# Attention tower on one core: every product on 64 rows by 32 columns of TensorE, and a step of an attend and of a piece beside each pair of scores

## What is computed

```python
h = gelu(layernorm(x.reshape(8, 1500, 80) @ W.T + b) * gamma + beta)      # 256 features
z = layernorm(h)
Q, K, V = (z @ W.T + b for each of q, k, v), split into 16 heads of 16 features
attn = softmax(Q @ K.T / 4)                                               # 1500 x 1500 for each head
h = h + (attn @ V) @ Wo.T + bo
out = h + layernorm(layernorm(h)) * ln_g + ln_b                           # the expert layer: 8 // 16 = 0 tokens a head
```

## Time and profile before

| | us |
|---|---|
| median of 3 runs | 2458.41 |
| the profiled execution's own time | 2458.36 |
| its span | 2456.6 |
| TensorE busy | 2237.6 |
| ScalarE busy | 2155.3 |
| VectorE busy | 920.3 |
| GpSimd busy | 371.5 |

### The profile page before, as it was taken

The page is one execution under the profiler, slowest core; times in us unless marked ns, Lnnn a source line. Parts: engine busy times, 40 slices in busy tenths (PEclk is TensorE's granted clock), DMA queues, the critical chain, the costliest instruction groups (busy, mean ns, idle before and its releaser), DMA issues.

```text
span 2456.6 us, 47924 instructions
## 1 busy us (share of the span) xinstructions
PE 2237.6 (91%) x19500; PEld 669.8 (27%) x19500; DVE 920.3 (37%) x2075; ACT 2155.3 (88%) x2332; POOL 371.5 (15%) x495
## 2 busy tenths in 40 slices
PE   4589999999999999999999999999999999998892
PEld 1222223222232223222232222322222222222221
DVE  7442235432354334532345233542335332330114
ACT  0098999989999899998999899998999989999991
POOL 2211102211021111210112110211112110110002
PEclk7799999999999999999999999999999999999996
DMA  2311221222112222212212221222222122111101
GB/s 71 107 37 40 66 67 41 57 66 65 50 40 66 64 66 49 57 48 58 74 40 52 70 66 40 50 62 60 69 54 50 41 65 67 47 44 39 33 6 32
DMA packets 109922, 133.62 MB, mean 54 GB/s; under 512 B 32263, under 2 KB 89670, under 8 KB 109694
## 3 DMA queue, kind: packets, MB, share of 16 engines
q1 hardware_dynamic: 107158, 128.64, 20.8%
q10 hardware_dynamic: 2536, 1.83, 0.3%
HBM read 55.16 MB, written 61.44 MB: 47 GB/s over the span
## 4 chain that ended last, share of the span: by engine, by line
issue 47%; PE 27%; ACT 10%; POOL 8%; DVE 3%; POOLq 1%; DMA 1%; SPq 1%; DVEq 0%; ACTq 0%
PE PS L853 12%; PE PS L829 8%; PE PS L790 5%; ACT prob L489 4%; ACT prob L486 4%; POOL sq L380 2%; POOL Y L388 2%; ACT prob L494 2%; POOL rs L390 2%; POOLq L389 1%; PE PS L799 1%; PE PS L774 1%; DVE z L550 1%; DVE HL L568 1%; POOL rs L367 1%
## 5 line engine op out<-in xcount | busy, mean ns | idle before, releaser
L853 PE MATMUL PS<-prob,Vst 125*32 125x500 f32 x9216 | 1131.4, 593 | 0.2 <-ACT prob L489 0.2
L494 ACT ACTIVATE prob<-PS 125x1000 f32<-125x1000 f32 x768 | 776.4, 1011 | 135.9 <-PE PS L829 134.6
L829 PE MATMUL PS<-QA,KA 64*125 64x500 f16 x4608 | 769.0, 406 | 84.5 <-ACT prob L489 45.7
L486 ACT ACTIVATE prob<-PS 125x1000 f32<-125x1000 f32 x768 | 775.3, 1010 | 80.4 <-PE PS L829 80.3
L489 ACT ACTIVATE prob<-PS 125x1000 f32<-125x1000 f32 x768 | 784.4, 1021 | 0.0
L829 PEld LDWEIGHTS PS<-QA,KA 64*125 64x125 f16 x4608 | 255.9, 131 | 861.6 <-ACT prob L486 413.6
L853 PEld LDWEIGHTS PS<-prob,Vst 125*32 125x32 f32 x9216 | 219.6, 108 | 424.6 <-issue 242.5
L566 DVE TENSOR_SCALAR HL<-PS,b_qk 128x500 f16<-128x500 f32 x96 | 70.9, 739 | 504.1 <-PE PS L790 427.7
L790 PE MATMUL PS<-zT,w_qk 128*32 128x500 f32 x1536 | 197.4, 596 | 8.9 <-DVE Osb L611 7.6
L380 POOL TENSOR_TENSOR sq<-HL 128x2000 bf16<-128x2000 f16 x24 | 84.5, 3522 | 752.4 <-DVE HL L568 752.4
L611 DVE COPY Osb<-PS 128x500 f32<-128x500 f32 x96 | 65.0, 677 | 257.5 <-PE PS L853 257.5
(11 more groups left out here) (79 smaller groups left out, 955.0 us busy)
## 6 DMA issues: line engine op xcount, KB each, us to landing
qk_halves_scratch<-HL SPq DMA_DIRECT2D x384, 125.0 KB
QA<-qk_halves_scratch SPq DMA_DIRECT2D x64, 375.0 KB, 5.0
KA<-qk_halves_scratch SPq DMA_DIRECT2D x64, 375.0 KB, 7.2
oT<-On SPq DMA_DIRECT2D x384, 31.2 KB, 2.0
out<-Y SPq DMA_DIRECT2D x24, 500.0 KB
X<-in_x SPq DMA_DIRECT2D x8, 468.8 KB, 7.9
thin<-Osb SPq DMA_DIRECT2D x96, 7.8 KB
Den<-thin SPq DMA_DIRECT2D x96, 7.8 KB
```

What stands on the lines that cost most here:

```text
L486: act.activation(prob[0:T, 6 * p:6 * p + 2, :], PS[0:T, 0:2, 0:QC], ACT.Exp, scale=scl)\
L494: act.activation(prob[0:T, 6 * p + 4:6 * p + 6, :], PS[0:T, 4:6, 0:QC], ACT.Exp, scale=scl)\
L829: last = pe.matmul(PS[0:T, bank, 0:QC], KA[rows, G % 2, h // 2, t * T:(t + 1) * T], QA[rows, G % 2, h // 2, c * QC:(c + 1) * QC], start=Tr ...
L853: last = pe.matmul(PS[lo:lo + 2 * HD, 6 + n % 2, 0:QC], Vst[:, b % 2, t, g * HG + j, :], prob[0:T, (HG * t + j) % 12, :], start=(t == 0), ...
```

## The change

All products except the transpositions and the norm sums now use 64 rows by 32 columns of the array, so eight run at once. An attend becomes two **steps** of eight matmuls with 250 queries: in step 0 the upper 64 rows work on one half of the queries and the lower 61 on the other, each into its own bank, and in step 1 they change places. A projection becomes four steps (two input halves, two places), the values, the output and the token embedding two. Each of these results now lies in two banks, one half of its columns in each. The table counts **windows** of one pair of scores (24 in a unit) instead of rounds of three, and gives each step a window of its own. Scores use banks 0 to 3, two pairs; attends and pieces use 4 and 5 or 6 and 7 in turn. Two new semaphores, `s_ph` and `s_stp`, make the second step of an attend or piece wait for the first, which wrote the bank that it adds to.

TensorE:

```diff
-            def attend(n, t):
-                for j in range(HG):
-                    last = pe.matmul(PS[lo:lo + 2 * HD, 6 + n % 2, 0:QC], Vst[:, b % 2, t, g * HG + j, :],
-                                     prob[0:T, (HG * t + j) % 12, :], start=(t == 0), stop=(t == NT - 1))
-                last.then_inc(s_pv, 1)
+            def attend(n, t, step):
...
+                if step:
+                    pe.wait_ge(s_ph, at(s_ph, NT * n + t + 1))
+                elif NT * n + t > 0:
+                    pe.wait_ge(s_pv, at(s_pv, NT * n + t))
+                for lower in range(2):
+                    a = (step + lower) % 2
+                    rows = slice(64, T) if lower else slice(0, 64)
+                    for j in range(HG):
+                        lo = 2 * HD * j
+                        last = pe.matmul(PS[lo:lo + 2 * HD, bank + a, 0:QC // 2], Vst[rows, b % 2, t, g * HG + j, :],
+                                         prob[rows, (HG * t + j) % 12, a * QC // 2:(a + 1) * QC // 2],
+                                         start=(t == 0 and step == 0), stop=(t == NT - 1 and step == 1))
+                last.then_inc(s_pv if step else s_ph, 1)
...
-                    last = pe.matmul(PS[0:T, bank, 0:QC], KA[rows, G % 2, h // 2, t * T:(t + 1) * T],
-                                     QA[rows, G % 2, h // 2, c * QC:(c + 1) * QC], start=True, stop=not exact_max)
+                        last = pe.matmul(PS[lo:hi, bank, 0:QC], KA[rows, G % 2, h // 2, t * T + lo:t * T + hi],
+                                         QA[rows, G % 2, h // 2, c * QC:(c + 1) * QC], start=True, stop=not exact_max)
...
-                for r in range(PER):
-                    R = R0 + r
-                    if R > 0:
-                        pe.wait_ge(s_ex, at(s_ex, 3 * R))
-                    scores(n, 6 * r + 4, 2, exact_max)
-                    pe.wait_ge(s_ex, at(s_ex, 3 * R + 1))
...
+                for k in range(WIN):
+                    w = WIN * n + k
+                    if w > 0:
+                        pe.wait_ge(s_ex, at(s_ex, w))
+                    if k < WIN - 1:
+                        scores(w + 1, exact_max)
...
+                    if k >= 2:
+                        attend(n, (k - 2) // 2, k % 2)
+                    elif n > 0:
+                        attend(n - 1, NT - 1, k)
+                    beside(b, u, k)
```

The table (two of its lines), and VectorE's finish, which now comes three windows after the take:

```diff
+    OFFSETS = {"tok": (0, 1), "turn": (0,), "qk": (0, 1, 3, 4), "val": (0, 1), "norm": (0,), "flag": (0,), "out": (0, 1)}
+    place(6, "qk", (4, 5), (11, 6), (18, 7))
+    place(7, "val", (4, 4), (7, 5), (10, 6), (13, 7))
...
+                            take_out(pb, i)
+                            finish.append((k + 3, pb, i))
```

The start and the end of the program. Before the first unit only four pairs of banks rotate, and the sums over the weights wait until the tokens are out of PSUM; after the last unit VectorE finishes one tile behind the take:

```diff
+                    pe.wait_ge(s_free, at(s_free, NT // 2))
...
-                for e in range(4, 8):
-                    take_out(B - 1, e, USE["out", B - 1, e] % 6)
-                    finish_out(B - 1, e)
-                invert(B * NU - 1)
-                normalise(B * NU - 1)
-                for e in range(8, NT):
-                    take_out(B - 1, e, USE["out", B - 1, e] % 6)
-                    finish_out(B - 1, e)
+                for e in range(CT, NT):
+                    take_out(B - 1, e)
+                    if e > CT:
+                        finish_out(B - 1, e - 1)
+                    if e == CT + 1:
+                        invert(B * NU - 1)
+                    if e == CT + 2:
+                        normalise(B * NU - 1)
+                finish_out(B - 1, NT - 1)
```

More of the change, by code:

```diff
@@ L11, in audio_tower @@
     RF, D = tok_wT.shape
+    RH = RF // 2
     NT, T = x.shape[2], x.shape[3]
@@ L27, in audio_tower @@
     BOUND = 60.0
[L28 to L89, removed]
+    WIN = NT * HG // 2
+    assert NU == NT and WIN == 24 and KR == 64
+    OFFSETS = {"tok": (0, 1), "turn": (0,), "qk": (0, 1, 3, 4), "val": (0, 1), "norm": (0,), "flag": (0,), "out": (0, 1)}
+    PLAN = {(u, k): [] for u in range(NU) for k in range(WIN)}
+    def place(u, what, *at):
+        for k, i in at:
+            for step, off in enumerate(OFFSETS[what]):
+                PLAN[u, k + off].append((what, i, step, step + 1 == len(OFFSETS[what])))
@@ new lines, in audio_tower @@
+    place(0, "out", (4, 4), (9, 5), (19, 6))
+    place(0, "tok", (14, 2))
+    place(1, "out", (4, 7), (14, 8))
+    place(1, "tok", (9, 3), (19, 4))
+    place(2, "out", (4, 9), (14, 10), (19, 11))
+    place(2, "tok", (9, 5))
+    place(3, "turn", (4, 0), (6, 1))
+    place(3, "qk", (9, 0), (16, 1))
+    place(4, "qk", (4, 2), (14, 3))
+    place(4, "val", (11, 0), (21, 1))
+    place(5, "val", (4, 2), (7, 3))
+    place(5, "turn", (10, 2), (12, 3))
+    place(5, "norm", (14, 0))
+    place(5, "qk", (16, 4))
@@ new lines, in audio_tower @@
+    place(6, "qk", (4, 5), (11, 6), (18, 7))
+    place(7, "val", (4, 4), (7, 5), (10, 6), (13, 7))
+    place(7, "turn", (16, 4), (18, 5))
+    place(7, "norm", (20, 1))
+    place(8, "qk", (4, 8), (11, 9), (18, 10))
+    place(9, "qk", (4, 11))
+    place(9, "val", (11, 8), (14, 9), (17, 10), (20, 11))
+    place(10, "norm", (4, 2))
+    place(10, "flag", (8, 0))
+    place(10, "tok", (12, 0), (18, 1))
+    place(11, "out", (4, 0), (9, 1), (14, 2), (19, 3))
+    assert all(len(steps) < 2 for steps in PLAN.values())
@@ new lines, in values @@
+            def values(b, i, step, swap):
+                bank, t = pair(USE["val", b, i]), (i % CT) * T
+                begin("val", b, i, step)
+                for c in range(KC):
+                    for lower in range(2):
+                        j = (swap + lower) % 2
+                        rows = slice(64 * lower, 64 * lower + 64)
+                        for lo, hi in blocks(T):
+                            last = pe.matmul(PS[lo:hi, bank + j, 0:D // 2], zT[rows, c, t + lo:t + hi],
+                                             w_v[rows, c, j * D // 2:(j + 1) * D // 2], start=(step == 0 and c == 0),
+                                             stop=(step == 1 and c == KC - 1))
+                end("val", b, i, step, last)
@@ new lines, in output @@
+            def output(b, e, step, swap):
+                bank = pair(USE["out", b, e])
+                if step == 0:
+                    pe.wait_ge(s_os, at(s_os, 64 * (b * NU + (NG - 1) * NC + e // CT + 1)))
+                begin("out", b, e, step)
+                for c in range(KC):
+                    for lower in range(2):
+                        j = (swap + lower) % 2
+                        rows = slice(64 * lower, 64 * lower + 64)
+                        for lo, hi in blocks(T):
+                            last = pe.matmul(PS[lo:hi, bank + j, 0:D // 2], oT[rows, c, e * T + lo:e * T + hi],
+                                             w_o[rows, c, j * D // 2:(j + 1) * D // 2], start=(step == 0 and c == 0),
+                                             stop=(step == 1 and c == KC - 1))
+                end("out", b, e, step, last)
```

479 lines of the change are left out of this document (256 added, 223 removed).

## The result

The changed kernel takes **2652.66 us** (median of 4 runs, 2637.40 to 2657.69), where the kernel before takes 2457.94 (4 runs): ratio 1.078, 95% interval 1.076 to 1.080. It is slower by 195 us where I forecast faster by 173. The profiled execution has a span of 2654.8.

What follows compares the result with a forecast made beforehand. TensorE and ScalarE equally loaded, TensorE's late scores costing 210 us. Start 120, gelus and table loads 35, exponentials 2041, lateness 50 and end 37 made a 2283 span, plus 1.8 outside: 2285 us, range 2245 to 2410.

Steps and rivals of the forecast that it cites:

- More instructions: TensorE's 1568 rows a unit, at 6 ns a row as in a burst, hide behind the array; cost set at nothing.
- Rows cost more than they fill: Rival: TensorE's sequencer can't keep up, deciding from 15 ns a row; 2570 us at 16 ns; 0.20 including too-dear row halves.
- Instruction supply: Cost of feeding TensorE the added matmuls and weight loads; the forecast set it at nothing.
- Small steps: Steps in adjacent windows make scores late: 0.24 us free, 19 us for qk, 24 for val, out and tok.
- Waits: New semaphore waits are over in time; bank waits set at nothing; SyncE keeps its DMA order, extra X loads hidden.
- a piece waits for VectorE to take the one before: A unit's pieces share one pair of banks; VectorE is 37% busy, so this wait was set at nothing.
- The start: Before the first exponential: later weight sums and four pairs of banks cost 3 us, bounds 0 and 10; first exponential at 120.
- The end: From last exponential to the span's end: finishing one tile behind cuts 54 us to 37, bounds 33 and 54.
- One shape everywhere: TensorE's 16 shape-change gaps a unit go, except around turns and norms; an eight-matmul half attend takes 0.42 us.
- No eight at a time: Rival: the row halves don't overlap in fp32, a step costs 0.84, 3410 us; 0.20 together with too-dear rows.
- Still TensorE: Rival: each step costs 0.05 to 0.1 us more than half an attend; 2367 us, range 2330 to 2430; chance 0.20.
- the rounds' 210 us: TensorE's lateness in the exponential stage of the kernel before, 210 us; the forecast left 50 of it.

Runs made afterwards that it cites:

- the first lap: Supply-only run without the kernel's work: 4096 TensorE instructions on eight 64x32 tiles, 64 fp16 columns, beside the output's zero writes; 57.5 us.
- the rebuilt kernel: Changed kernel with one-step attends, values and outputs in a bank per row half, pieces laid out anew, finish, division, gelu and SyncE issues moved; 2371.21 us, ratio 0.965.
- The fifth lap: Same supply-only run, 64 fp16 columns on eight tiles again, beside heavier transfers: 1684 instructions in 35 us with them, 1792 in 26 us without.
- laps 2 to 4: Same supply-only run: 500 fp16 columns, 300 fp32 columns, then whole 128x128 tiles with 64 columns; 59.5, 66.9 and 62.6 us.

## Why the prediction was wrong

**The step that failed** is *More instructions*: "I take the burst, as nothing in the waits is charged to issue except the change of shape, and set it at nothing". The supply was neither the 57 ns proven long in the earlier trace rows nor the 6 ns of the earlier trace rows, but a third thing that no row of before could show under load: bursts at 5 to 6 ns from a store of some 450 instructions, and 14 to 15 ns over the long run, 21 beside heavy transfers. The step had its own threshold, "hides behind the array while it stays under 14 ns", and the measured value lies on it. The rival *Rows cost more than they fill* named the mechanism and its point (15 ns), but not the size: by its own sum a steady supply of 15 ns gives at most 96 x 1568 x 15 ns + 159, 2417 us, and 2652.66 came. Its sum goes by a unit's average, and the instructions come in windows of 48, 80 and 112, with no more than some 450 held ahead; and other terms failed beside it. The chance of 0.19 for slower was too small for a term whose two bounds lay a factor of nine apart, on either side of the threshold. The prediction did not weigh the rule that bears on this: the Trainium skill ("Runtime: NRT & Kernel Launch", section "Instruction fetch mechanics") says that instructions come in blocks of 256 and calls the fetch hidden, as the sequencer issues slower than blocks arrive. The blocks of 256 agree with the trace; that the fetch is hidden does not, by the pauses of 2.45 us in the first lap above.

Against the forecast's span of 2283 the profile has 2654.8, 372 more:

- *Instruction supply*, set at 0: 201 us of lateness lie within 2.5 us behind a pause at a 256th row.
- *Small steps*, 43 us in 432 second steps of 0.10: the medians are 0.15 to 0.19 each, so about 0.17 x 432 = 73, **30 more**. Mechanism right, size off.
- *Waits*: "The SyncE order keeps its DMAs" was wrong where it mattered. The order of issue was kept, but the token piece that the load of `X` waits for was moved from unit 1 to unit 2, and the sums' transfer stood behind it: 35.8 us at the gelus, set at 0. Taken away, it gave 44.
- "a piece waits for VectorE to take the one before ... I set this at nothing": not covered where VectorE itself stands at a transfer. Units 3 and 5 have medians of 3.1, 1.5 and 2.3 us at single windows, unit 9 1.0; with smaller ones this may be most of the 90 us that the other items leave. I have this from the place of the waits; only its part at the gelu, in unit 2, was tested by removal, so the rest is argued and not shown.
- *The start*, 3 us (bounds 0 and 10): the first exponential came at 130.80, 13.7 later than before and outside the bounds. The weight sums run at 33.49 instead of 18.86, 14.6 later; I took only their length and not that the whole chain of scales behind them shifts.
- *The end*, 37 (33 to 54): 39.2 measured, 40.1 on the kernel before. Right.
- *One shape everywhere*: right in each part. Steps of eight matmuls on two row halves take half an attend, no gap of 0.14 us is left between scores and attends, and without pieces ScalarE has all of its time. *No eight at a time* is out. *Still TensorE* is out in its size: in the timeline at 1201 us one step follows another after 0.42 to 0.45. Whether the 0.07 more of a second step are a dearer step or less free lateness than the 0.24 taken was not separated.

One more sum shows what the change gave. All lateness of the exponentials, the gelus' 35 us in it, is 443 us after and 244 before. Behind pauses at a 256th row lie 201 of it after and some 5 before. What is left, about 240, is the same in both: what the smaller steps should have won back of the rounds' 210 us went again, by the items above, to the gelus, the second steps and the waits for VectorE.

The first and last exponential after (the weight sums on line 992, the last pair on ScalarE, the last store):

```profile
33.49 3.75 PE L992 MATMUL PS<-prob,ones 128*128 128x512 f32 x4 [9.59 <-DVE Hs L525]
...
130.80 3.69 ACT L488 ACTIVATE prob<-PS 125x1000 f32<-125x1000 f32 x4 [93.96 <-PE PS L879]
...
2613.66 1.90 ACT L488 ACTIVATE prob<-PS 125x1000 f32<-125x1000 f32 x2 [0.23 <-PE PS L879]
...
2629.56 16.59 SPq L286 DMA_DIRECT2D out<-Y  x3
```

The forecast of 2285 took it that all pieces fit; the rebuilt kernel at 2371 shows how far that goes with this tiling and 1056 rows a unit.

## What to carry to other kernels

Count an engine's instructions per microsecond, not only its busy time: before cutting matmuls into more tiles, divide the time by the number of loads and matmuls, for the stage and for its densest windows, and look at the instruction queue's packets. Here 22 ns a row was fine, and 18.4 was fine where every window had the same 48 rows. 17.9 with windows of 80 and 112 rows went with some 200 us of lateness behind pauses, and at 15.4 such lateness was three quarters of all. When a step is moved, follow every in-order queue whose next entry waits for it, first of all the queue that issues transfers. Place the work of a pipeline so that each window's sum fits and a buffer's taker has its time before the next user; the same tiling gave 2653 and, with fewer instructions and pieces laid out so, 2371 us.

## What the runs showed of the hardware

- TensorE's instructions come in packets of 256; with none to spare a packet starts every 3.45 to 3.9 us, also beside 133 GB/s of transfers, and every 5.7 us beside 282 GB/s, and each pause ends some 1.4 us after the packet's landing. After a long wait 446 stood ready.
- Between different 64x32 tiles instructions start 5 ns apart (256 in 1.28 us), loads included. 2048 loads and matmuls of one whole tile with 64 columns took 62.6 us, some 30 ns a pair, without a pause.
- The fifth lap of 64 columns ran at a granted clock of 0.50 (1.2 GHz) throughout, after TensorE had stood for 26.5 us, as it had before laps 2 to 4, which ran at 0.95 to 1.00. The supply was no slower for it: 14.5 ns once the transfers were over.
- One VectorE instruction of 0.48 us (line 647) took 2.41 us in unit 3 of the second batch, beside one of GpSimd of 2.52 us; it was seen once and not tested.
